# One recurrence step on VectorE: the first stage squares the unclipped q, its local term is written as two accumulator columns, and p is added to four rows in one instruction

## The reference, cut to what matters

```python
def _derivative(q, p, drive, coupling, bias):
    i_couple = jnp.tanh(q) @ coupling.T
    dq = q - q ** 3 / 3.0 - p + drive + i_couple + bias
    dp = EPSILON * (q + ALPHA - BETA * p)
    return dq, dp

def _rk4_step(q, p, drive, coupling, bias):
    dq1, dp1 = _derivative(q, p, ...)
    dq2, dp2 = _derivative(q + 0.5 * DT * dq1, p + 0.5 * DT * dp1, ...)
    dq3, dp3 = _derivative(q + 0.5 * DT * dq2, p + 0.5 * DT * dp2, ...)
    dq4, dp4 = _derivative(q + DT * dq3, p + DT * dp3, ...)
    q_next = jnp.clip(q + DT / 6.0 * (dq1 + 2 * dq2 + 2 * dq3 + dq4), -20, 20)
    p_next = jnp.clip(p + DT / 6.0 * (dp1 + 2 * dp2 + 2 * dp3 + dp4), -20, 20)

# q of all steps -> x;   w_gu, w_down: 4-bit codes times scales of groups of 128
gate, up = split(x @ w_gu.T)             # 512 -> 2 x 1408
y = (silu(gate) * up) @ w_down.T         # 1408 -> 512
out = x_in + y / sqrt(mean(y * y) + 1e-6)
```

## Time and profile before

| what | us |
|---|---|
| median of 3 runs | 1540.77 (1540.26 to 1540.93) |
| the profiled execution, its own time | 1541.22 |
| its span, first to last instruction | 1539.4 |
| PE busy / PEld busy | 1461.3 / 1415.1 |
| DVE busy | 1414.1 |
| ACT busy | 735.1 |
| first and last reduce L694 of the recurrence start at | 54.4 and 1500.6 |

### The profile page before, as it was taken

How to read it: one execution, slowest core, us unless ns; L and a number is a source line. 1 busy time by engine, 2 the same in 40 slices (tenths; PEclk the granted TensorE clock), 3 DMA queues, 4 the chain that set the end, 5 groups by cost and what they waited for, 6 DMA issues and landing times.

```text
span 1539.4 us, 90592 instructions
## 1 busy us (share of the span) xinstructions
PE 1461.3 (95%) x37025; PEld 1415.1 (92%) x37025; DVE 1414.1 (92%) x10250; ACT 735.1 (48%) x5607; POOL 21.3 (1%) x45
## 2 busy tenths in 40 slices
PE   2678999999999999999999999999999999999998
PEld 0467999999999999999999999999999999999998
DVE  7999999999999999999999999999999999999991
ACT  3344444454454444445445444545444454444541
POOL 0100000000000000000000000000000000000000
PEclk9999999999999999999999999999999999999999
DMA  9100000000000000000000000000000000000000
GB/s 228 38 7 14 7 4 7 21 7 4 24 4 21 7 11 18 4 24 4 21 8 11 18 4 25 4 21 7 4 24 4 24 4 21 7 4 24 4 21 21
DMA packets 11940, 28.39 MB, mean 18 GB/s; under 512 B 1537, under 2 KB 5889, under 8 KB 11393
## 3 DMA queue, kind: packets, MB, share of 16 engines
q1 hardware_dynamic: 11520, 22.57, 5.6%
q10 hardware_dynamic: 2, 0.03, 0.0%
HBM read 18.40 MB, written 4.19 MB: 15 GB/s over the span
## 4 chain that ended last, share of the span: by engine, by line
PE 69%; DVE 21%; ACT 5%; issue 2%; POOLq 0%; DVEq 0%; POOL 0%; ACTq 0%
PE scan_ps L567 41%; PE gu_ps L312 17%; PE y_ps L324 11%; DVE th L642 3%; ACT th L605 3%; DVE scan_ps L694 3%; DVE scan_ps L661 2%; DVE p_part L636 2%; DVE with_q L636 2%; ACT t L607 2%; DVE q_cub L656 2%; DVE q_raw L694 1%; DVE with_p L636 1%; DVE scan_ps L696 1%; DVE q_sq L646 1%
## 5 line engine op out<-in xcount | busy, mean ns | idle before, releaser
L567 PE MATMUL scan_ps<-th,wscan 128*128 128x32 f16 (+1 forms) x32768 | 1038.3, 174 | 37.1 <-ACT th L605 23.4
L567 PEld LDWEIGHTS scan_ps<-th,wscan 128*128 128x128 f16 x32768 | 956.5, 96 | 70.4 <-ACT th L605 32.0
L605 ACT ACTIVATE th<-scan_ps 128x16 f16<-128x16 f32 x1536 | 281.5, 183 | 568.5 <-DVE scan_ps L694 568.2
L312 PE MATMUL gu_ps<-hist,wffn 128*128 128x128 f32 x2816 | 503.4, 284 | 0.0
L312 PEld LDWEIGHTS gu_ps<-hist,wffn 128*128 128x128 f32 x2816 | 394.0, 192 | 0.0
L642 DVE TENSOR_TENSOR th<-t,th 128x16 f16<-128x16 f32 x2048 | 309.4, 172 | 49.6
L324 PE MATMUL y_ps<-wffn,h 128*128 128x128 f32 x1408 | 324.1, 313 | 0.5 <-DVE h L340 0.5
L607 ACT ACTIVATE t<-scan_ps 128x16 f32<-128x16 f32 x1536 | 273.5, 178 | 0.0
L324 PEld LDWEIGHTS y_ps<-wffn,h 128*128 128x128 f32 x1408 | 209.6, 189 | 1.1 <-DVE h L340 1.1
L390 ACT ACTIVATE sum_r<-dr,constant 128x64 f32<-128x64 f32 x528 | 184.0, 351 | 17.2 <-DMA dr<-drive 17.2
L605 ACT ACTIVATE th<-q_raw 128x16 f16<-128x16 f32 x512 | 106.1, 207 | 174.1 <-DVE q_raw L694 164.1
(11 more groups left out here) (41 smaller groups left out, 567.0 us busy)
## 6 DMA issues: line engine op xcount, KB each, us to landing
raw<-packed SPq DMA_DIRECT2D x11, 768.0 KB, 10.2
dr<-drive SPq DMA_DIRECT2D x34, 128.0 KB, 3.0
xres<-x SPq DMA_DIRECT2D x16, 256.0 KB, 3.5
out<-osb SPq DMA_DIRECT2D x16, 256.0 KB, 2.8
coup<-coupling_t SPq DMA_DIRECT2D x1, 1024.0 KB, 12.6
sc<-scales ACTq DMA_DIRECT2D x1, 33.0 KB
q_raw<-cond_t SPq DMA_DIRECT2D x1, 16.0 KB, 5.6
bias<-bias_t SPq DMA_DIRECT2D x1, 2.0 KB, 6.7
```

Source lines behind the costliest of these rows:

```text
L312: i = nc.tensor.matmul(gu_ps[b][:, half * P:(half + 1) * P], wffn[:, u, j * P:(j + 1) * P], hist[1 - f.parity][:, kt].rearrange("p t b -> ...
L567: i = nc.tensor.matmul(to if both else to[:, 0], wscan[:, w, part, kt, cols], moving if both else moving[:, 0], start=first, stop=last, sk ...
L605: nc.scalar.activation(th[s % 2][:, c, 0, :], q, ACT.Tanh, scale=1.0 / S).then_inc(now.tanh_hi, 1)
```

## The change: what it does, and the diff

`q_sq` of stage 0 is made from `q_raw` in place of the clipped q, with the sign turned, and a `max` in `cube_first` limits it to the square of the clip's bound (to a very large number in the first step, where q is not clipped). `cube_first` no longer subtracts from a linear factor; it writes the cube's term straight into the local slots 2 and 5 of PSUM. A new `linear_first` writes the linear term (own factor times q plus with_p's row 0) into two more slots, 3 and 4. The second half's slots move so that each half has four slots in a row, and stage 0's two reduces add four slots instead of three. `local_in` is not called in stage 0; both new writers increment `first_half`, so that its count rises by one more in each step. `add_p` of stage 0 makes four rows at once, and the one-row call at the head of stage 1, with the wait behind it, goes. The square stands between the two low parts, and the wait for the clip moves from the square to `linear_first`.

```diff
+UNLIMITED = 1e20
...
-LOCALS = STEPS * 18
+LOCALS = STEPS * 16
...
         for half in range(2):
-            slots = scan_ps[:, half * 5 * APART:(half * 5 + 3) * APART].rearrange("p (k r) -> p k r", k=3)
-            own = slots[:, :, 0:HB]
-            wide_prod.append(slots[:, half:half + 2, 0:COPIES * HB].rearrange("p k (r e) -> p k r e", r=COPIES))
-            three.append(own.rearrange("p k (c b) -> p c b k", b=B))
+            slots = scan_ps[:, half * 4 * APART:(half + 1) * 4 * APART].rearrange("p (k r) -> p k r", k=4)
+            own = slots[:, :, 0:HB].rearrange("p k (c b) -> p c b k", b=B)
+            wide_prod.append(slots[:, 2 * half:2 * half + 2, 0:COPIES * HB].rearrange("p k (r e) -> p k r e", r=COPIES))
+            three.append(own[:, :, :, half:half + 3])
+            four.append(own)
         middle = scan_ps[:, 2 * APART:8 * APART].rearrange("p (h r) -> p h r", h=2)
         local_ps = middle[:, :, 0:HB]
+        linear_ps = scan_ps[:, 3 * APART:5 * APART].rearrange("p (h r) -> p h r", h=2)[:, :, 0:HB]
...
-            def square_first(q):
-                return local(nc.vector.scalar_tensor_tensor(q_sq[:, :, :], q, CUBE[0], q, ALU.mult, ALU.mult))
-
-            def cube_first(q):
-                return local(nc.vector.scalar_tensor_tensor(q_cub[:, :, :], q_sq[:, :, :], OWN[0], q,
-                                                            ALU.subtract, ALU.mult))
+            def square_first():
+                return local(nc.vector.scalar_tensor_tensor(q_sq[:, :, :], q_raw[:, :, :], -CUBE[0], q_raw[:, :, :],
+                                                            ALU.mult, ALU.mult))
+
+            def cube_first(q, limit):
+                nc.vector.scalar_tensor_tensor(local_ps.rearrange("p h (c b) -> p h c b", b=B),
+                                               quarters(q_sq[:, :, :]), -CUBE[0] * limit ** 2, quarters(q),
+                                               ALU.max, ALU.mult).then_inc(now.first_half, 1)
+
+            def linear_first(q):
+                nc.vector.scalar_tensor_tensor(linear_ps.rearrange("p h (c b) -> p h c b", b=B),
+                                               quarters(q), OWN[0], quarters(with_p[:, 0]),
+                                               ALU.mult, ALU.add).then_inc(now.first_half, 1)
...
-                dve.wait_ge(now.first_half, 2 * s + 2)
-                nc.vector.tensor_reduce(q_half(following, 0), three[0], AX.X, ALU.add).then_inc(now.q_ready, 1)
+                slots = three if i else four
+                dve.wait_ge(now.first_half, 2 * s + 2 + s // 4 + 1)
+                nc.vector.tensor_reduce(q_half(following, 0), slots[0], AX.X, ALU.add).then_inc(now.q_ready, 1)
                 dve.wait_ge(now.second_half, s + 1)
-                nc.vector.tensor_reduce(q_half(following, 1), three[1], AX.X, ALU.add).then_inc(now.q_ready, 1)
+                nc.vector.tensor_reduce(q_half(following, 1), slots[1], AX.X, ALU.add).then_inc(now.q_ready, 1)
...
-                add_p(t, 0, 3)
+                rows = add_p(t, 0, 4)
...
+                low_part(s, 0)
+                squared = square_first()
+                low_part(s, 1)
                 if t:
                     dve.wait_ge(now.clipped, t)
                 elif before:
                     dve.wait_ge(before.clipped, STEPS)
-                squared = square_first(q1)
-                low_part(s, 0)
-                low_part(s, 1)
+                dve.wait_ge(now.local, rows)
+                linear_first(q1)
                 dve.wait_ge(now.local, squared)
-                cubed = cube_first(q1)
+                cube_first(q1, CLAMP * S if t or before else UNLIMITED)
                 add_q(with_q1[0], 1, BY_Q1, q1, with_p[:, 1])
-                dve.wait_ge(now.local, cubed)
-                local_in(s)
                 add_q(with_q1[1], 2, BY_Q1, q1, with_p[:, 2])
                 finish(s)
...
-                row3 = add_p(t, 3, 1)
                 add(p_part[0][:, :, :], p_state[:, :, :], P_SUM[0], q1)
-                dve.wait_ge(now.local, row3)
                 add_q(with_q1[2], 3, BY_Q1, q1, with_p[:, 3])
```

More of the change, by code:

```diff
@@ L261, in program @@
         y_ps = [ctx.enter_context(nc.psum_tensor(f"y_ps{i}", [P, N], F32)) for i in range(2)]
-        wide_prod, three = [], []
+        wide_prod, three, four = [], [], []
         for half in range(2):
-            slots = scan_ps[:, half * 5 * APART:(half * 5 + 3) * APART].rearrange("p (k r) -> p k r", k=3)
-            own = slots[:, :, 0:HB]
-            wide_prod.append(slots[:, half:half + 2, 0:COPIES * HB].rearrange("p k (r e) -> p k r e", r=COPIES))
-            three.append(own.rearrange("p k (c b) -> p c b k", b=B))
+            slots = scan_ps[:, half * 4 * APART:(half + 1) * 4 * APART].rearrange("p (k r) -> p k r", k=4)
[3 more added lines that the diff above has]
+            four.append(own)
         middle = scan_ps[:, 2 * APART:8 * APART].rearrange("p (h r) -> p h r", h=2)
         local_ps = middle[:, :, 0:HB]
+        linear_ps = scan_ps[:, 3 * APART:5 * APART].rearrange("p (h r) -> p h r", h=2)[:, :, 0:HB]
         q_stage = [middle[:, :, (4 + i) * HB:(5 + i) * HB] for i in range(3)]
@@ L277, in halves, with quarters @@
             return tile.rearrange("p (h c) b -> p h (c b)", h=2)
+        def quarters(tile):
+            return tile.rearrange("p (h c) b -> p h c b", h=2)
         scan_in = sem("scan_in")
@@ L623, in dve_block @@
         def dve_block(dve, now, before, ffn, rest):
-            linear = [with_p[:, 0], with_q1[0][:, :, :], with_q2[0][:, :, :], with_q3[:, :, :]]
+            linear = [None, with_q1[0][:, :, :], with_q2[0][:, :, :], with_q3[:, :, :]]
             count = [0]
```

## The result

| | before | changed |
|---|---|---|
| median, us | 1540.51 (4 runs, 1540.13 to 1540.93) | 1483.09 (4 runs, 1481.48 to 1483.74) |
| profiled span, us | 1539.4 | 1479.7 |

The ratio is 0.9626 (95% interval 0.9609 to 0.9642): 57 us gained where 47 were forecast, 1483 in place of 1494.

What follows compares the result with a forecast made beforehand. Stage 0, and stage 1 barely, were taken to wait for VectorE's late first low part. Gains of 0.165 + 0.017 = 0.182 us a step, times 256, 46.6 us, gave 1494 us; range 1483 to 1512.

Steps and rivals of the forecast that it cites:

- The hole behind the twelfth matmul, and VectorE's order as its cause: Stage 0: loads pause (0.14 us hole) because the first low part stands behind clip and square; moving it gains 0.185 us.
- PSUM in place of SBUF: Stage 0's cube and linear term: PSUM writes cost nothing in the sum, at worst 15 ns each.
- +0.51, plus stage 3's 0.85, +1.36: Stage 0 on TensorE: first load at +0.51 us plus stage 3's 0.85 us of work puts the next reduce at +1.36.
- 1.53 for stage 0 before: Time from stage 3's first reduce to stage 0's in one step, the base for stage 0's forecast gain of 0.165 us.
- 0.01 added for a second wait: Stage 0's linear term waits for two semaphores; priced at 0.01 us between nothing and 0.11, giving the reduce at +1.365.
- Stages 2 and 3 ... nothing: Stages 2 and 3 hold the same instructions and already run at 0.85 us or close to it: no gain.
- stage 1 as 0.017: Stage 1: TensorE limits the gain to 0.023 us, none in the quarter with a third product; mean 0.017 us.
- the low part sets both stages: Stages 0 and 1 before: first low part to next reduce is 0.72 and 0.73 us, so the low part sets both.
- That of VectorE's queue: Rival: second wait or PSUM writes hold VectorE 0.11 us more in stage 0; gain 21 us, 1520 us; chance 0.16.
- TensorE's floor: Rival: four-slot reduce free, stage 0 and two-product stage 1s both at 1.34 us; gain 56 us, 1485 us; chance 0.10.
- The reduce at half rate: Rival: stage 0's four-slot reduces take 0.217 us more each, delaying stage 1; 12 us slower, 1553 us; chance 0.04.
- the full TensorE: Rival: TensorE is full at 97%, so an earlier low part only moves its wait; no change, 1541 us; chance 0.04.

Runs made afterwards that it cites:

- e1: Kernel before the change, with only stage 0's first low part moved ahead of the square and its wait for the clip: 1490.24 us, ratio 0.9677 to the kernel before.
- e3: Changed kernel with stage 0's first low part put back behind the square, so both low parts follow it: 1506.81 us, 24 us above the changed kernel.
- e8: Changed kernel with stage 0's first low part moved ahead of the clip too: 1496.57 us, 13 us slower than the changed kernel.
- e10: Changed kernel with stage 0's square taken from the clipped q again, behind its wait for the clip: 1487.9 us, 5 us above the changed kernel.
- e7: Changed kernel with one more 128x32 VectorE instruction, output unused, ahead of stage 0's first reduce: 1486.81 us, 3.7 us above the changed kernel.
- e12: Changed kernel with two more 128x32 VectorE instructions, outputs unused, ahead of stage 3's first reduce: 1507.71 us, 25 us lost.
- e4: Changed kernel with stage 0's cube to SBUF, local term behind a wait for it, three-slot reduces, no limit on the square: 1494.53 us, 11 us above the changed kernel.

## Why the prediction was right in kind and short in size

*The hole behind the twelfth matmul, and VectorE's order as its cause*: right, and shown by e1 and e3. The low part came to +0.61 (forecast +0.625), the linear term to +0.90 (+0.915), the four-row addition took 281 ns, the four-slot reduce 233 (forecast 235; groups view of the changed kernel):

```profile
L643 DVE SCALAR_TENSOR_TENSOR with_p<-p_state,sum_r 128x128 f32<-128x128 f32 x226 | 63.5, 281 | 0.0
L709 DVE TENSOR_REDUCE scan_ps<-scan_ps 128x16 f32<-128x64 f32 x225 | 52.3, 233 | 0.0
```

*PSUM in place of SBUF*: the two new writers take 193 and 194 ns and start 0.10 apart (775.39, 775.49, 775.59), so nothing was lost. The estimate of 65 ns more that the prediction took from the Trainium skill (Perfetto Trace Analysis, section Optimizing Scalar/DVE Operations) is not borne out here.

*"+0.51, plus stage 3's 0.85, +1.36", and 1.53 for stage 0 before.* This term was mis-sized. Stage 0 gave 0.195 on the mean, not 0.165. 0.019 of the difference is in the base, since one step's 1.53 stood for a mean of 1.549. The other 0.011 is about the 0.01 added for a second wait: the reduce does not come after VectorE's queue, whose last row starts at +1.21 and the reduce at +1.34. TensorE's 0.85 was too long for this stage as well; its run took 0.83 (775.00 to 775.83). The 0.85 was read from stage 3, where the first load starts at +0.49 and 0.056 us pass before the second; the fifth starts at +0.62 in either stage. What ends stage 0 was not on the list: its second low part, shown by e8 and e10.

*"Stages 2 and 3 ... nothing", and stage 1 as 0.017.* This step failed. Stage 1's period hardly moved, for VectorE's queue became what its reduce waits for (777.11, then 777.21). I had looked only at TensorE there and not summed the queue of that stage. This queue hangs on the stage's second low part, at +0.76, and that on the second tanh, complete at +0.73, so that an instruction fewer ahead of the first low part brings it nothing. It was close before, too: the last row started at +1.26 and the reduce at +1.38, so "the low part sets both stages" held for stage 1 by a margin of about 0.01 us. Yet TensorE lost nothing by it and stage 2 gave the time back: 0.007 came from stage 1 and 0.029 from stage 2, 0.036 together where 0.017 was forecast, 0.019 a step or 5 us more. It is the give-back of e7; e12 shows that it is not general. With stage 0's 0.03 a step (8 us) this makes the profile's own 59 us in place of 47, and by the medians the missing 10 us.

*The rivals.* That of VectorE's queue did happen, in stage 1 rather than in stage 0, and without its price. TensorE's floor, 1485 us, was nearest in time: its 1.34 came true for stage 0. The first load did come at +0.51, as was held against it, but that costs nothing, since the feed-forward loads fill that time and the fifth load is at +0.62 as in stage 3. The reduce at half rate and the full TensorE did not come.

No experiment with the whole computation was faster than the changed kernel.

## What to carry to other kernels

When several engines are above 90% busy, compare stages that do the same work and look for the hole in the longest one; a single instruction moved ahead of another that waits can be most of a change. Measure a stage on the engine that sets it, and ask what the next stage hangs on: a late first reduce was paid back where the next stage follows TensorE and the second reduce, and not where it follows the first reduce alone. Edits are not additive: four rows at once was worth nothing on the kernel before and 10 us on top of the moved low part.

## What the runs showed of the hardware that was not expected

A wait for two semaphores cost VectorE next to nothing where both had been given: the changed kernel's linear term, with two, starts 0.092 us after the second low part, and e10's, with one, 0.085. Where the second had not, it was dear: in e4 the cube starts 0.10 us behind the square's completed write, with one wait (e1) 0.03. And an additional instruction that delays a reduce by 0.065 us a step, 17 us in 256 steps, cost 3.7 us, while two at another place that delay it by 0.116 us, 30 us in all, cost 25: the place decides more than the length.
